# Order of the first tiles' VectorE steps, two matmul blocks ahead of a merge, drains of GpSimd in the expert loop, and one clear of the semaphores

## What is computed

```python
h = _layernorm(x) * (1 + ca) + sa
# memory layer; x_in is 64 memory rows, then h
out_swa = _swa(x_in, wq, wk, wv, wo)
def loss_fn(params):                      # _mlp: silu(x @ w1.T + b1) @ w2.T + b2
    return 0.5 * jnp.sum((_mlp(*params, k_flat) - v_flat) ** 2)
grads = jax.grad(loss_fn)((w1, b1, w2, b2))
upd = tree_map(lambda p, g: (1.0 - alpha) * p - theta * g, (w1, b1, w2, b2), grads)
out_mem = _mlp(*upd, k_flat)
merged = sigmoid(out_swa @ lin1.T) * out_swa + sigmoid(out_mem @ lin2.T) * out_mem
x = x + ga * merged[:, NUM_PM:, :]
h = _layernorm(x) * (1 + cb) + sb
gates = softmax(h @ wg.T); w_topk, idx_topk = top_k(gates, 8); w_topk /= sum(w_topk)
# buf[e, rank]: the rows of expert e, at most CAPACITY = 160
out = einsum('ecf,ehf->ech', x1 * silu(x2), expert_w2)    # x1, x2 halves of buf @ expert_w1.T
x = x + gb * (_swiglu(h, shared_w1, shared_w2) + combined) # combined: out's rows times weight, added by row
```

## Time and profile before

| | us |
|---|---|
| median of 3 timed runs (lowest, highest) | 1960.25 (1959.46, 1963.38) |
| the profiled execution | 1961.02 |
| its span, first to last instruction | 1959.0 |

### The profile page before, as it was taken

The page is one execution under the profiler, slowest core; times in us unless marked ns, Lnnn a source line. Parts: engine busy times, 40 slices in busy tenths (PEclk is TensorE's granted clock), DMA queues, the critical chain, the costliest instruction groups (busy, mean ns, idle before and its releaser), DMA issues.

```text
span 1959.0 us, 35930 instructions
## 1 busy us (share of the span) xinstructions
PE 1901.6 (97%) x12384; PEld 1696.3 (87%) x12384; DVE 1043.7 (53%) x2262; ACT 830.0 (42%) x1661; POOL 933.6 (48%) x667
## 2 busy tenths in 40 slices
PE   7999999999999999999999999889999999999996
PEld 5888888888888887687877787789999999999996
DVE  7877777777777776676666777212112122122121
ACT  6666666666666665453354453111111111112111
POOL 4665666566666662056666666462222222222322
PEclk9999999999999999999999999899999999999998
DMA  6211111111111103121101110567777877877774
GB/s 219 68 37 34 36 33 36 36 45 40 36 36 35 50 11 107 33 75 53 34 12 44 43 33 1 184 198 241 265 254 254 271 251 253 273 246 260 241 262 138
DMA packets 104279, 233.83 MB, mean 119 GB/s; under 512 B 20676, under 2 KB 84891, under 8 KB 96032
## 3 DMA queue, kind: packets, MB, share of 16 engines
q1 hardware_dynamic: 79648, 220.48, 32.2%
q0 software_dynamic: 24576, 12.69, 4.3%
HBM read 194.56 MB, written 78.45 MB: 139 GB/s over the span
## 4 chain that ended last, share of the span: by engine, by line
PE 58%; another core or an unknown queue 2%; DVE 0%; issue 0%; ACT 0%; POOLq 0%; ACTq 0%; POOL 0%; DVEq 0%
PE bank L1860 32%; PE bank L82 19%; PE bank L1147 4%; PE bank L2032 1%; PE bank L1995 1%; PE bank L1643 1%; POOLq L2067 0%; DVE early L1522 0%; DVE b_h_low L1425 0%; DVE c_gT L1955 0%; DVE b_g L1509 0%; DVE b_g L1511 0%; ACT early L1328 0%; ACT b_h_high L1322 0%
## 5 line engine op out<-in xcount | busy, mean ns | idle before, releaser
L1955 DVE TENSOR_TENSOR c_gT<-bank,c_sil 128x480 f32<-128x480 f32 x128 | 84.2, 658 | 559.1 <-PE bank L1860 521.8
L1837 POOL DMA_INDIRECT slots<-b_row,b_index x224 | 250.0, 1116 | 201.0 <-issue 120.2
L1972 POOL DMA_INDIRECT out_rows<-c_y,c_x x96 | 134.3, 1398 | 350.3 <-DMA out_rows<-c_y,c_x 180.5
L1860 PE MATMUL bank<-c_gT,c_w 128*128 128x160 f32 x1536 | 226.6, 304 | 12.6 <-DVE c_gT L1955 10.7
L1860 PEld LDWEIGHTS bank<-c_gT,c_w 128*128 128x128 f32 x1536 | 213.9, 192 | 13.9 <-DVE c_gT L1955 10.0
L1860 PE MATMUL bank<-c_xT,early 128*128 128x160 f32 x1536 | 221.4, 301 | 1.9 <-issue 1.9
L1860 PE MATMUL bank<-c_xT,c_w 128*128 128x160 f32 x1536 | 220.0, 300 | 0.0
L1860 PEld LDWEIGHTS bank<-c_xT,early 128*128 128x128 f32 x1536 | 213.2, 191 | 2.7 <-issue 2.6
L1860 PEld LDWEIGHTS bank<-c_xT,c_w 128*128 128x128 f32 x1536 | 212.3, 191 | 0.0
L1932 ACT ACTIVATE c_sil<-bank 128x480 f32<-128x480 f32 x128 | 73.1, 571 | 289.8 <-PE bank L1860 268.4
L439 POOL TENSOR_TENSOR last_row<-last_row,a_e 128x256 f32<-128x256 f32 x33 | 54.4, 1649 | 129.4 <-DVE a_e L694 127.7
(11 more groups left out here) (317 smaller groups left out, 4911.7 us busy)
## 6 DMA issues: line engine op xcount, KB each, us to landing
c_w<-in_e2T SPq DMA_DIRECT2D x64, 768.0 KB
c_w<-in_e1T SPq DMA_DIRECT2D x32, 1536.0 KB
early<-in_e1T SPq DMA_DIRECT2D x31, 1536.0 KB
slots<-a_fill SPq DMA_DIRECT2D x16, 642.0 KB
c_x<-slots SPq DMA_DIRECT2D x48, 200.6 KB
a_x_in<-in_x SPq DMA_DIRECT2D x32, 128.0 KB, 2.0
xT_tiles<-a_xT SPq DMA_DIRECT2D x32, 128.0 KB
swaT_tiles<-a_swaT SPq DMA_DIRECT2D x32, 128.0 KB
```

Of the source, the lines that this page charges most:

```text
L1837: pool.indirect_dma_start(out=T["slots"], out_offset=bass.IndirectOffsetOnAxis(ap=index[:, t, k:k + 1], axis=0), in_=row[:, t, :], in_offs ...
L1860: return nc.tensor.matmul(out, lhsT, rhs, start=first, stop=last, skip_group_check=True)
L1955: dve.tensor_tensor(flat(gT[p][:, g * H:(g + 1) * H, :]), psum[2 + 2 * g][:, 0:H * CAP], flat(sil[:, g * H:(g + 1) * H, :]), ALU.mult).the ...
L1972: pool.indirect_dma_start(out=T["out"], out_offset=bass.IndirectOffsetOnAxis(ap=token, axis=0), in_=y[q % 2][:, h, :], in_offset=None, bou ...
```

## The change

1. In tile 0 VectorE takes six of the twelve inverse-square-root steps ahead of its body; the other six and the offset come behind `prec`.
2. In tile 1 the statistics of chunk 4 come behind `prec` instead of ahead of it.
3. In tile 0 the second modulation copy and the two rate steps come behind the low parts of w2T and h instead of ahead of them.
4. In the token stage two of the eight first-layer blocks of chunk 1 are issued by TensorE behind chunk 0's lin2 and ahead of the transposes that wait for chunk 0's merge. Chunk 0's lin2 writes banks 7 and 2.
5. In the loop over the experts GpSimd waits for `added` with an instruction of its own at q = 0 (experts 4, 8, ..., 60), and drains behind it.
6. The semaphores of both prefixes are cleared by one call: before, the end has 17 clearing instructions on GpSimd in two groups, each group with its meeting of all engines; now it has one and one meeting.

```diff
-    def clear(self):
+    def clear(self, *others):
-        self.nc.clear_and_free_semaphores(list(self.made.values()))
+        self.nc.clear_and_free_semaphores([s for sems in (self, *others) for s in sems.made.values()])
         self.nc.all_engine_barrier()
...
-def inverse_sqrt(dve, done, calls, y, var, t):
+def inverse_sqrt(dve, done, calls, y, var, t, part=range(RSQRT_OPS)):
...
-    for k, op in enumerate(ops):
-        op().then_inc(done, 1)
+    for k in part:
+        ops[k]().then_inc(done, 1)
         dve.wait_ge(done, calls * RSQRT_OPS + k + 1)
...
-                if known(n, 1) and not known(n, 2):
-                    statistics(4)
-                elif known(n, 2) and not known(n, 3):
+                if known(n, 2) and not known(n, 3):
...
                 dve.reciprocal(prec[:], psums[:]).then_inc(S("prec"), 1)
+                if known(n, 1) and not known(n, 2):
+                    statistics(4)
                 if first:
+                    deviations(0, (0,), range(6, RSQRT_OPS))
                     modulation(0)
...
-                if first:
-                    modulation(1)
-                    dve.wait_ge(S("rates_in"), 32)
-                    dve.tensor_scalar(keep[:], alpha[:], -1.0, 1.0, ALU.mult, ALU.add)
-                    dve.tensor_scalar(step[:], theta[:], -1.0, None, ALU.mult).then_inc(S("rates"), 1)
                 for g in range(2):
...
+                if first:
+                    modulation(1)
...
-            deviations(0, (0,))
+            deviations(0, (0,), range(6))
             tiles(dve, body)
...
+    AHEAD = 2
+    LIN2_BANK, LIN2_FIRST = (7, 0), (7, 2)
...
-        def body(c, after, last=False):
+        def hidden_layer(c, after, js):
             if after:
                 pe.wait_ge(S("xT_low"), c)
-            for j in range(HC):
+            for j in js:
...
+        def body(c, after, last=False, begun=0):
+            hidden_layer(c, after, range(begun, HC))
...
+            if not after:
+                hidden_layer(1, True, range(AHEAD))
             pe.wait_ge(S("merged"), c + 1)
...
-        body(1, True)
+        body(1, True, begun=AHEAD)
...
-            wait_past(pool, S("added"), n * 32)
+            if q == 0 and not isinstance(n, int):
+                wait_apart(pool, S("added"), n * 32, S("passed_pool"))
+                pool.drain()
+            else:
+                wait_past(pool, S("added"), n * 32)
...
-            tokens.clear()
-            experts.clear()
+            tokens.clear(experts)
```

16 lines of the change are left out of this document (10 added, 6 removed).

## The result

| | before | after |
|---|---|---|
| median of 5 timed runs (lowest, highest), us | 1961.58 (1959.46, 1963.38) | 1949.11 (1948.21, 1951.21) |
| the profiled execution, us | 1961.02 | 1949.71 |
| its span, us | 1959.0 | 1947.9 |

What follows compares the result with a forecast made beforehand. TensorE, 97% busy, was taken as the bound, with gains only where it waits. −0.2 − 2.9 − 5.1 + 0.5 − 2.25 = −9.95 took 1961.0 to 1951.05, or 1950.3 us on the median's basis; range 1946.5 to 1957.0.

Steps and rivals of the forecast that it cites:

- the end's drain: Kernel end: GpSimd's last drain outlasts the landing by 5.1 us, 13 ns for each of 384 DMAs; gain 5.1.
- the seam: Token stage, chunks 0 and 1: twelve matmuls fill TensorE's 3.21 us idle ahead of the transposes; gain 2.9, ends 1.4 and 3.2.
- the tiles: Tiles 0 and 1: moved VectorE steps gain 0.2 us together, nothing from tile 0 and 0.2 from tile 1.
- the drains in the loop: Expert loop: fifteen GpSimd drains, the first 3.4 us and the others 0.1 each, cost 0.5 in all.
- R3: Rival, chance 0.15: each loop drain costs 5.1 us past a landing and slows the loop; 1966, within 1958 to 1977.
- the sign that would have told against the forecast: Expert loop: a change of its length by over 2 us would show the forecast wrong.
- R2: Rival, chance 0.20: the end's drain keeps its 5.1 us whatever ran before; 1955.4.
- the 1.26 ahead of `prec`: Tile 0: moving seven small VectorE steps frees at most 1.26 us, of which 1.0 reaches `prec`.
- the end of the second w2T low part: Tile 0: VectorE's second w2T low part ends no earlier than GpSimd lets it, at about 31.4 as before.
- The lock: Tile 0: GpSimd's use of the shared port holds VectorE's moved two-SBUF-operand steps, most until 20.6; 0.6 us lost.
- R4: Rival, chance 0.14: GpSimd doesn't hold small VectorE steps, so tile 0 gains 1.6 us; 1948.7.
- The clear: Kernel end: two clears with 17 range clears become one range and one barrier; gain 2.25 us, ends 2.0 and 2.6.

Runs made afterwards that it cites:

- one_drain: The kernel before with one single GpSimd drain added in front of the expert loop, behind the landing of expert 3's rows; ratio 1.0000 to before.
- tiles: The kernel before with only parts 1 to 3 of the change (all that concerns tiles 0 and 1); ratio 0.9994 to before.
- drains: The kernel before with only part 5, a GpSimd drain at experts 4, 8, ..., 60; ratio 0.9978 to before.
- curve: The kernel before with GpSimd's expert steps written out and drains only at experts 4, 5, 7, 13, 27 and 61; timed once, 1957.4 us.
- seam: The kernel before with only part 4, two first-layer blocks of chunk 1 issued ahead of chunk 0's merge; ratio 0.9980 to before.
- late_drain: The kernel before with GpSimd's expert steps written out and one single drain, at expert 60; ratio 0.9979 to before.
- clear: The kernel before with only part 6, one clear for both semaphore prefixes; ratio 0.9992 to before.
- part1: The kernel before with only part 1, six inverse-square-root steps and the offset of tile 0 moved behind `prec`; timed once, 1935.4 us.
- full: The whole change, run in the second session against the kernel before; median 1948.44 against 1961.98 us, ratio 0.9924.
- early_s2: The whole change plus the conversion of the shared expert's second weights moved ahead of chunk 0's lin2; median 1947.98 us, ratio 0.9924 to before.
- base: The kernel before, unchanged, profiled again in the second session; timed once, 1964.6 us.
- part3: The kernel before with only part 3, tile 0's second modulation copy and two rate steps behind the w2T low parts; timed once, 1938.7 us.

## Why the prediction was right, and where not

The time came out inside the range, and the two largest terms, the end's drain and the seam, were right. That it came within 1.2 of the single figure is luck in part: the tiles gave 2.2 more than their term and the drains in the loop cost 0.5 less, the clock took 1.4, and the median of before had been taken 1.3 too low. One sum is off without consequence: R3's lower end, 15 lags of 0.4 less 5, makes 1956.4 and not 1958.

**The end's drain, −5.1: right in size (4.84 in the first pair, 4.3 with an interval of 2.7 to 6.1 alone), wrong in its law.** The step that failed is the division of 5.1 by 384. Each DMA of GpSimd costs the next drain 82 ns and not 13, but the sum stops near 6. By that law one drain ahead of the loop would have left 120 × 13 ns = 1.6 of the 5.1; it left 5.0 (one_drain). What saved the forecast is that 8 are few by either law. The 5.1 behind the landing are the last part of 7.0 us from the end of GpSimd's last issue (1948.16) to the end of its drain; with 8 DMAs this is 2.2, with 120 it is 6.8.
**The drains in the loop, +0.5: no cost.** The first took 5.947 where 3.4 was put down, and the others 0.70 for 0.1; but the lag that they make, up to 6.5, never reaches TensorE, and at the end y sets the issue again (0.43 behind y in both traces of the first pair). From the y of expert 4 to that of expert 63 it is 618.9 with and without them, so the sign that would have told against the forecast stayed away. R3 fails at its first condition: a drain behind a landing costs by the count since the last one, and with 8 it is 0.7, under the 0.9 from which R3 decides, and that only if none of it were free.
**R2 falls** with the drain's 0.3 behind the landing. The prediction set a sentence of the Trainium skill against this drain ("VectorE: DVE Perf Modes", section "The DRAIN you can't avoid"). That sentence gives some 12 ns for the boilerplate drains ahead of and behind a kernel; the ones here are the program's own, and the rows have them from 0.041 to 9.58 us on GpSimd, so it decides nothing about R2.
**The tiles, −0.2: wrong, −2.4 in the first pair and 2.3 in the mean of the traces.** Two steps failed. First, of the 1.26 ahead of `prec` I let 1.0 through; it became 2.03. 1.21 came through whole, the w1T low parts took 2.35 instead of 2.88 besides, because they now begin ahead of GpSimd's L413 rather than behind its start, and VectorE's wait for TensorE fell by 0.3, as TensorE's matmuls come up to speed 2.5 earlier than in the first trace of before. The eight traces of the unchanged stage differ by 1.0 in `prec` among themselves, so how much of this 0.3 is the change's isn't separated. Second, the end of the second w2T low part was held fixed at 31.4, "no earlier than GpSimd lets it". It ended at 29.40: the idle of 1.66 that stood ahead of the pair was gone, and GpSimd's own work had moved up too. e gained 1.95 by both; the rest of the 2.4 arises by tile 2's `prec` (71.89 to 69.48), where 0.2 was put down, and how much of it is tile 1's own step and how much the clock's isn't separated. The lock itself was as said: the moved steps hit L420, one of 0.16 took 1.75, and R4 falls with it. But the lock held one step, for 1.75, and the six around it ran at their 0.13 to 0.16; and what waits for GpSimd moves when GpSimd does. The exclusive lock that the Trainium skill describes ("SBUF — State Buffer", section "SBUF: two separate sides") agrees with this row of 1.75 too, and tile 0 gained what R4 had, and more, all the same.
**The seam, −2.9: right.** 2.73 in the first pair, the new wait for L1556 at the place where it was put (1.27 for 1.2), the transposes at 1.09 for 1.05, the routing step at 812.83 where the forecast's 813.4, less the 0.74 that had arrived at lin2, makes 812.7. Its range was too small on the good side: the gain is up to 5.0 where the clock falls late and stays at 0.50 for 6.8 us, of which the trace of before showed only the milder form with 3.4.
**The clear, −2.25: right** (2.45).
**What was not in the sum** is TensorE's clock behind idle times that the change doesn't touch. In the profiled execution of the change it took 1.7 at the start of the token stage and 0.2 at the entry of the expert stage (1.0 given, 1.3 taken), and it gave 0.5 near the end of the token stage, where of the two only the trace of before has 3.4 us at 0.50 (from 1206): 1.4 in all. Over the fourteen traces the way from the token stage's first matmul to lin2, the same matmuls each time, takes 27.00 to 28.70, and it takes more in step with how long the clock stands at 0.50: 2.8 to 3.0 us of it in before, tiles, drains and curve (27.0 to 27.1), 3.4 in seam, one_drain, late_drain and clear (27.3), 4.4 in part1 and full (27.7) and in early_s2, which has one more step of ScalarE on this way (27.9), 5.6 in base (28.3), 5.7 in part3 (28.4), 6.2 in after (28.7). The prediction counted each gain as arriving whole. In one execution it needn't, and two executions of one kernel differ by as much: the spans of base and of the first trace of before by 3.9 us.

## What to carry to other kernels

If GpSimd issues many small DMAs and its drain at the end outlasts the last landing, one earlier drain can take the time off the end, but only if few DMAs follow it: with 8 behind it (late_drain) it did as much as fifteen drains, with 120 behind it (one_drain) nothing. It costs some 6 us of GpSimd's own time, which must be free there; four experts from the end 0.7 of it was left. When a step is moved on an engine that shares something with another, follow the other engine's times along with it; an end that "waits for GpSimd" is not a fixed time. A gain of 2 us read from one pair of traces should be set against the spread of the unchanged kernel's traces, 1.3 us in this stage one. And a gain of 2 us ahead of an idle of TensorE should be read in the rows ahead of that idle, since the clock behind it can give or take as much from one execution to the next.

## What the runs showed of the hardware

- A drain of GpSimd costs 0.04 + 0.082 us for each indirect DMA (an add of 80 rows) that GpSimd issued since its last drain, measured for 2 to 68 of them, and far less for more: 5.591 for 68, 5.947 for 264, 6.151 for 376, all with every DMA landed. The values repeat to the nanosecond between executions (5.947 for 264 in after, full, one_drain, drains, curve and early_s2), and nearly so for 8 (0.704 for the second drain of the loop, 0.699 for the others).
- A VectorE step of 128x4 with two SBUF inputs takes 1.75 instead of 0.16 when GpSimd has begun a multiplication of 1.93 ahead of it; the two steps before it, begun in the same stretch (17.52 and 17.68), took 0.13 and 0.16.
- Behind the same idle of TensorE, 2.27 us at the start of the token stage, the granted clock stands at 0.50 for 2.8 us in one trace of the kernel before and for 5.6 in another; over all traces it is 2.8 to 6.2. Behind an idle of 3.21 us it was already at 0.50 when the work began again (before), or fell only 1.2 us later (base).
- The same kernel took 1937.9 in one session and 1962 in two others. 17 to 21 of the 24 us lie at the entry of the expert stage: from the first gated product to the y of expert 4 it is 52.8 in the four traces of the first session and 70.2 to 73.8 in the other ten, with TensorE busy for 94.2 and 79.2 us in the same window of 95 (tiles and base). From there to the y of expert 63 it is 618.9 in before and in tiles.
